# Sampling weights of a deformable convolution: the hats go through DRAM and are spread by DMA, not by selector products

## The chip, the cores and the metric

One core of a Trainium2 chip runs the whole program. The metric is the device time of one execution in microseconds; below is better.

## The reference, cut to what matters

The input is 16 images of 64 channels, 16 x 16 pixels. Four blocks follow each other: (0) a channel attention, x + softmax(q kT / 8) v with a 64 x 64 matrix for each image; (1) a modulated deformable 3 x 3 convolution with batch norm and ReLU; (2) a pixel attention with a 256 x 256 softmax for each image; (3) a block of layer norm, depthwise 3 x 3 convolution, four gated 1-D depthwise scans, a fuse product, a second layer norm and a gated feed-forward part.

The change is about block 1. For each of nine taps and each output pixel it samples the image at a fractional place:

```python
py = off_y + hh[None, None, :, None] + ky[None, :, None, None] - PAD
px = off_x + ww[None, None, None, :] + kx[None, :, None, None] - PAD
sampled = jax.vmap(_bilinear_sample_one)(x, py, px)
sampled = sampled * mask[:, None]
out = jnp.einsum('bckhw,ock->bohw', sampled, w_dcn.reshape(O, C, KK))
```

Bilinear interpolation with zeros outside is the same as a product of two "hats": the weight of source pixel (i, j) is max(0, 1 - |py - i|) * max(0, 1 - |px - j|). So for each tap the kernel builds a matrix of weights, 256 source pixels by 256 output pixels for each image, and lets TensorE multiply it with the image that has already been multiplied with the tap's channel weights.

## The kernel before, in words

Two images make a pair: their 2 x 64 channels fill the 128 partitions, and there are eight pairs. Every pair walks through the same named steps, and a step is written `name.pair`. Each engine works through one written list of steps (`PLAN`), in that order, and waits on semaphores; the lists interleave the steps of several pairs. So an engine's order is fixed, and a step that waits holds everything behind it in its list.

Front steps of pair n: `qk`, `attn`, `at`, `mix`, `x1` (block 0), `off` and `off_t` (offsets, transposed so that pixels are partitions, lines 430 to 447), `wx0` to `wx2` (image times tap weights, line 480). On VectorE `dist` (line 872), on ScalarE `abs`, on VectorE `hat` and `hat_y` make the hats: for each output pixel (a partition) 18 rows of 16 values, y and x for nine taps.

Then the hats must come to the layout that the products need: source pixel as partition, output pixel along the row. Before the change this goes so. ScalarE rounds the hats to fp16 (`high`, line 710), GpSimd computes the low part, again fp16 (`low`, line 1039, for the first pair partly on VectorE, line 891). TensorE transposes both in fp16 (`tr0` to `tr2`, line 464), ScalarE copies them out of PSUM (line 719). For each tap k the step `sp{k}` (lines 504 to 519) makes three products with constant 0/1 selector matrices: two spread the y hats over the partitions, one for each half of the source rows (line 494, banks `yb`), and one spreads the x hats (line 489, bank `xb`). ScalarE copies the x part to SBUF (`xe{k}`, line 740) and VectorE multiplies, once for each half (`w{k}a`, `w{k}b`, line 901). TensorE then accumulates the samples (`s{k}a`, `s{k}b`, line 534) in the bank `cv`, and ScalarE writes the ReLU (line 747). Weights live in a ring of six tiles, the copies of x in three.

Back steps: `qk2`, `v2`, `logit`, `max`, `exp`, `nrm`, `et`, `av` (block 2), then `x3`, `st1`, `ln1`, nine taps `dw` (two on ScalarE, seven on VectorE, line 942), `y`, `gate`, `scan` (line 615), `prod` (line 957), `fuse`, `x4`, `st2`, `ln2`, `ff`, `u`, `ff2`, `out` (block 3). GpSimd computes the layer norms' scale and shift.

The PSUM banks `mb` and `pair` are shared by many steps; `turn` makes a step wait until the one before it in the same bank was read. `warm` and `hot` are products of a zero tile that nobody reads, put where TensorE would wait; `WARM` and `HOT` say how many pairs of them. SP issues the loads of parameters and of x, and the stores of y.

## Time and profile before

| | |
|---|---|
| median of 3 timed runs | 303.65 us (303.19 to 303.67) |
| span of the profiled execution | 301.8 us; its own time is not listed, the median run lies 1.9 us above this span |
| TensorE busy | 287.8 us (95%), 2870 matmuls |
| TensorE weight loads | 183.7 us (61%), beside the matmuls |
| VectorE busy | 213.0 us (71%), 424 instructions |
| ScalarE busy | 190.4 us (63%), 399 instructions |
| GpSimd busy | 53.0 us (18%), 139 instructions |
| DMA | 4.98 MB in all, mean 16 GB/s |
| granted TensorE clock | full speed (2.4 GHz) in all 40 slices |

Busy time is the union of an engine's instructions in the span. Matmuls are pipelined, so that one lasts longer than the time until the next can start: what a step costs a full TensorE is read from the start of the next step, or from the chain of waits, which goes back from the last instruction to what released each piece.

### The profile page before, as it was taken

The page shows a single profiled execution, that of the slowest core. Times are in us where ns is not written, and L with a number is a line of the kernel's source. Part 1 is how long each engine was busy: PE and PEld are TensorE (multiplying, and loading weights), DVE is VectorE, ACT ScalarE, POOL GpSimd, SP SyncE. Part 2 cuts the span into 40 slices and gives each one's busy share as a digit, 9 for nine tenths or more (in the row PEclk, how much of TensorE's full clock was granted, in tenths as well). Part 3 has the DMA queues.
Part 4 walks back from the last instruction along what each step waited for, and adds up shares of the span by engine and source line. Part 5 has one row for each costly group of instructions (what it writes and reads, how often), then busy time and mean ns, then how long its engine had stood idle before and what let it go on. Part 6 is the DMA issues. An engine that isn't in the chain of part 4 may idle for free.

```text
span 301.8 us, 7399 instructions
## 1 busy us (share of the span) xinstructions
PE 287.8 (95%) x2870; PEld 183.7 (61%) x2870; DVE 213.0 (71%) x424; ACT 190.4 (63%) x399; POOL 53.0 (18%) x139
## 2 busy tenths in 40 slices
...
DMA packets 3057, 4.98 MB, mean 16 GB/s; under 512 B 336, under 2 KB 2768, under 8 KB 2896
## 3 DMA queue, kind: packets, MB, share of 16 engines
...
## 4 chain that ended last, share of the span: by engine, by line
PE 85%; DVE 5%; ACT 5%; issue 3%; POOL 1%; ACTq 0%; POOLq 0%; DVEq 0%
PE ps_cv L534 22%; PE ps_pair L615 11%; PE ps_yb L494 8%; PE ps_pair L480 7%; PE ps_ma L437 6%; PE ps_ma L464 4%; PE ps_mb L580 3%; PE ps_pair L602 3%; PE ps_pair L570 3%; PE ps_mb L591 3%; PE ps_mb L547 3%; PE ps_mb L388 2%; PE ps_pair L635 2%; PE ps_mb L624 2%; PE ps_yb L374 1%
## 5 line engine op out<-in xcount | busy, mean ns | idle before, releaser
L901 DVE TENSOR_TENSOR sb_wt<-ps_yb,sb_xe 128x512 f32<-128x512 f32 x144 | 94.0, 684 | 26.4 <-PE ps_xb L489 24.9
L534 PE MATMUL ps_cv<-sb_wt,sb_w_x 128*64 128x256 f32 x576 | 77.3, 385 | 0.0
L740 ACT ACTIVATE sb_xe<-ps_xb 128x512 f32<-128x512 f32 x72 | 43.0, 597 | 19.3 <-PE ps_xb L489 19.2
L534 PEld LDWEIGHTS ps_cv<-sb_wt,sb_w_x 128*64 128x64 f32 x576 | 38.2, 136 | 20.2 <-issue 7.5
L615 PE MATMUL ps_pair<-sb_y_pad,sb_par 64*128 64x256 f32 x320 | 37.4, 383 | 0.3 <-ACT sb_gates L799 0.3
L615 PEld LDWEIGHTS ps_pair<-sb_y_pad,sb_par 64*128 64x128 f32 x320 | 30.9, 184 | 5.8 <-issue 2.5
L942 DVE SCALAR_TENSOR_TENSOR sb_dw_acc<-sb_z_pad,sb_par,sb_dw_acc 128x256 f32<-128x256 f32 x56 | 25.2, 480 | 9.4 <-ACT sb_dw_acc L792 5.3
L494 PE MATMUL ps_yb<-sb_hats,sb_sel 32*128 32x512 f16 x144 | 29.8, 383 | 0.7
L1039 POOL TENSOR_TENSOR sb_parts<-sb_hat,sb_parts 128x256 f16<-128x256 f32 (+2 forms) x40 | 23.3, 615 | 38.7 <-ACT sb_parts L710 38.6
L1046 POOL TENSOR_SCALAR sb_sc<-sb_mv 128x1 f32<-128x1 f32 x16 | 3.0, 190 | 142.1 <-DVE sb_mv L936 74.7
L489 PE MATMUL ps_xb<-sb_hats,sb_sel 32*128 32x512 f16 x72 | 27.7, 385 | 0.2 <-ACT sb_hats L719 0.2
L730 ACT ACTIVATE sb_w_x<-ps_pair 128x1024 f32<-128x1024 f32 (+1 forms) x24 | 19.4, 810 | 7.7 <-PE ps_pair L480 7.5
L480 PE MATMUL ps_pair<-sb_par,sb_x 64*128 64x256 f32 (+1 forms) x192 | 23.4, 361 | 0.6 <-ACT sb_w_x L730 0.3
L719 ACT ACTIVATE sb_hats<-ps_ma 128x1024 f16<-128x1024 f16 (+1 forms) x24 | 21.1, 880 | 1.7 <-PE ps_ma L464 1.5
L494 PEld LDWEIGHTS ps_yb<-sb_hats,sb_sel 32*128 32x128 f16 x144 | 7.3, 91 | 21.2 <-issue 17.0
L480 PEld LDWEIGHTS ps_pair<-sb_par,sb_x 64*128 64x128 f32 x192 | 15.5, 185 | 7.3 <-issue 6.7
L808 ACT ACTIVATE sb_conv<-ps_pair,sb_par 128x512 f32<-128x512 f32 x16 | 10.1, 683 | 13.1 <-PE ps_pair L615 13.0
L437 PE MATMUL ps_ma<-sb_x_pad,sb_par 128*64 128x128 f32 x288 | 17.4, 274 | 0.3 <-ACT sb_hats L719 0.3
L437 PEld LDWEIGHTS ps_ma<-sb_x_pad,sb_par 128*64 128x64 f32 x288 | 15.8, 136 | 2.3 <-issue 1.6
L769 ACT ACTIVATE sb_b_exp<-ps_pair,sb_b_neg 128x256 f32<-128x256 f32 x32 | 14.8, 473 | 3.0 <-DVE sb_b_neg L910 2.7
L872 DVE TENSOR_TENSOR sb_dist<-ps_ma,sb_grid 128x1152 f32<-128x1152 f32 x8 | 10.8, 1354 | 6.2 <-PE ps_ma L446 6.2
L464 PE MATMUL ps_ma<-sb_sel,sb_parts 128*64 128x128 f16 x320 | 13.8, 222 | 0.0
...
## 6 DMA issues: line engine op xcount, KB each, us to landing
sb_par<-in_par SPq DMA_DIRECT2D x1, 1519.5 KB, 7.7
sb_x_in<-in_x SPq DMA_DIRECT2D x8, 128.0 KB, 2.1
out_y<-sb_y_out SPq DMA_DIRECT2D x8, 128.0 KB, 1.7
...
sb_par<-in_par SPq DMA_DIRECT2D x1, 128.0 KB, 2.2
sb_sel<-in_sel SPq DMA_DIRECT2D x1, 128.0 KB, 3.9
```

What stands on the lines that cost most here:

```text
L437: mm = nc.tensor.matmul(ma[C * h:C * (h + 1), 0:P], par_sb[:, a + 2 * OM * t:a + 2 * OM * (t + 1)], x1_pad[:, r:r + HALF_ROWS, t % 3:t % 3 ...
L464: mm = nc.tensor.transpose(bk[columns_of(t), at:at + P], parts[:, 2 * h + b, 4 * g + 2 * t:4 * g + 2 * (t + 1), :, :], ident16)
L480: mm = nc.tensor.matmul(pair[:, 512 * b + PIX * h:512 * b + PIX * h + k], x1[r, P * h:P * (h + 1)], par_sb[r, a:a + k], start=True, stop=True)
L489: return nc.tensor.matmul(xb[:, :], sel_sb[rows, P:2 * P], hats[n % 2][rows, g, :], start=True, stop=True)
L494: return nc.tensor.matmul(yb[h][:, :], sel_sb[rows, P * (2 + h):P * (3 + h)], hats[n % 2][rows, g, :], start=True, stop=True)
L534: mm = nc.tensor.matmul(cv[C * b:C * (b + 1), 0:PIX], w_x[n % 2][:, b, h, k, :], wt_of(n, k, h)[:, PIX * b:PIX * (b + 1)], start=(k == 0 a ...
L615: mm = nc.tensor.matmul(pair[:, 512 * b + PIX * d:512 * b + PIX * (d + 1)], par_sb[r, a:a + P], rows, start=(j == 0), stop=(j == KS - 1))
L719: nc.scalar.activation(hats[n % 2][:, g0:g1, :].rearrange("p g q -> p (g q)"), ma[:, :].bitcast(F16)[:, 0:k], ACT.Copy).then_inc(ev(f"hats ...
L740: nc.scalar.activation(xe[t % XE][:, :], xb[:, :], ACT.Copy).then_inc(ev("xe_ok"), 1)
L901: nc.vector.tensor_tensor(wt_of(n, k, h)[:, :], yb[h][:, :], xe[t % XE][:, :], ALU.mult)\
L942: nc.vector.scalar_tensor_tensor(out=sum_of, in0=dw_source(t), scalar=col("dw_w", t), in1=sum_of, op0=ALU.mult, op1=ALU.add).then_inc(ev(f ...
L1039: nc.gpsimd.tensor_tensor(parts[:, 0:g, a:b, 1, :], hat[:, 0:g, a:b, :], parts[:, 0:g, a:b, 0, :], ALU.subtract).then_inc(ev("low_ok"), 1)
```

## The change

The low and high parts, the selector products, their constants (`in_sel`) and the copies of x go. Instead:

- `tr0` to `tr2` each transpose the f32 hats of three taps, 96 rows, in four blocks of 128 pixels; ScalarE copies them to SBUF in f32.
- SP gets a list of its own. `keep{g}` writes the 96 x 512 block of group g to a DRAM tensor of the program. `ld{k}` reads it back for tap k in three DMAs, each with a source that repeats rows, so that every one of 128 partitions gets a row of 512 f32: once the x hats, and twice (for each half) the y hats. Four such sets of buffers (`SPREADS`).
- `w{k}` is one VectorE product of 128 x 1024 for both halves, the x part broadcast. The ring has three tiles of twice the size.
- "Another layout": source pixels lie on the partitions with x slow and y fast, so that both spreads have an outer dimension of 16; GpSimd's copy of `x1` is permuted to match, in two pieces.
- The three banks that are free now go to a second `cv`, to a bank `mc` of its own for the back steps that shared `mb`, and to `rest` for the filler. Many tiles get a second buffer (`z_pad`, `dw_acc`, `y_pad`, `gates`, `conv`, `prod`, `z2`, `ff_*`), x4 a third, x2 one for each pair, and waits are written for their reuse.
- All lists are written anew.

```diff
-GROUPS = 5
-SLOT = 2 * H
+GROUPS = 3
+GROUP_TAPS = 3
+ROWS = 2 * H * GROUP_TAPS
...
-RING = 6
-HOT = {1: 4, 2: 2, 3: 3, 4: 2, 5: 5, 6: 5, 7: 8, 8: 13, 9: 4}
-WARM = {1: 5, 2: 2, 3: 5, 4: 1, 5: 3, 6: 2, 7: 3}
-XE = 3
+RING = 3
+SPREADS = 4
+HOT = {1: 6, 2: 1, 3: 1, 4: 1, 5: 1, 6: 2, 7: 1, 8: 4, 9: 1, 10: 3, 11: 3, 12: 2, 13: 2, 14: 1, 15: 2, 16: 18, 17: 3, 18: 3, 19: 8, 20: 3}
+WARM = {1: 7, 2: 2, 3: 4, 4: 1, 5: 1, 6: 1, 7: 1, 8: 4, 9: 1, 10: 2, 11: 1, 12: 1, 13: 1}
...
+            def keep(g):
+                def step(n):
+                    sp.wait_ge(ev(f"hats_ok{g}"), n)
+                    if n > 2:
+                        sp.wait_ge(ev("wt_ok"), tap(n - 2, GROUP_TAPS * (g + 1) - 1))
+                    sp.dma_start(hats_d[n % 2][g, :, :], hats[n % 2][:, g, :]).then_inc(kept[g][n % 2], 16)
+                return step
+
+            def spread(k):
+                def step(n):
+                    t, g, r = tap(n, k), k // GROUP_TAPS, 2 * H * (k % GROUP_TAPS)
+                    sp.wait_ge(kept[g][n % 2], 16 * ((n + 1) // 2))
+                    wait_past(sp, ev("wt_ok"), t - SPREADS)
+                    whole = [W, HALF_ROWS, 2 * PIX]
+                    rows = hats_d[n % 2][g, r + H:r + 2 * H, :]
+                    sp.dma_start(xs[t % SPREADS][:, :],
+                                 rows.unsqueeze(1).to_broadcast(whole)).then_inc(landed[t % SPREADS], 16)
+                    for h in range(HALVES):
+                        rows = hats_d[n % 2][g, r + HALF_ROWS * h:r + HALF_ROWS * (h + 1), :]
+                        sp.dma_start(ys[t % SPREADS][:, h, :],
+                                     rows.unsqueeze(0).to_broadcast(whole)).then_inc(landed[t % SPREADS], 16)
+                return step
...
-                    bk = ma[:, :].bitcast(F16)
-                    for g in range(g0, g1):
-                        for b in range(2):
-                            for h in range(HALVES):
-                                at = 2 * PIX * (g - g0) + PIX * b + P * h
-                                for t in range(2):
-                                    mm = nc.tensor.transpose(bk[columns_of(t), at:at + P],
-                                                             parts[:, 2 * h + b, 4 * g + 2 * t:4 * g + 2 * (t + 1), :, :],
-                                                             ident16)
+                    for b in range(2):
+                        for h in range(HALVES):
+                            at = PIX * b + P * h
+                            mm = nc.tensor.transpose(ma[0:ROWS, at:at + P],
+                                                     hat[:, 2 * h + b, 2 * GROUP_TAPS * g:2 * GROUP_TAPS * (g + 1), :], ident)
...
-            def weights(k, h):
+            def weights(k):
                 def step(n):
                     t = tap(n, k)
-                    dve.wait_ge(ev("sp_mm"), spread_of(n, k) + h)
-                    if h == 0:
-                        dve.wait_ge(ev("xe_ok"), t)
-                    wait_past(dve, ev("smp_mm"), slot(n, k, h) - RING)
-                    nc.vector.tensor_tensor(wt_of(n, k, h)[:, :], yb[h][:, :], xe[t % XE][:, :], ALU.mult)\
-                        .then_inc(ev("wt_ok"), 1)
+                    dve.wait_ge(landed[t % SPREADS], 48 * ((t - 1) // SPREADS + 1))
+                    wait_past(dve, ev("smp_mm"), 2 * (t - RING))
+                    nc.vector.tensor_tensor(wt_of(n, k)[:, :, :], ys[t % SPREADS][:, :, :],
+                                            xs[t % SPREADS][:, :].unsqueeze(1).to_broadcast([P, HALVES, 2 * PIX]),
+                                            ALU.mult).then_inc(ev("wt_ok"), 1)
                 return step
```

The parts of the new lists that the prediction speaks of. SP, the first two pairs:

```
load.3 keep0.1 keep1.1 keep2.1 ld0.1 ld1.1 ld2.1 ld4.1 load.4 ld3.1 ld6.1 keep0.2 ld5.1 ld7.1 load.5 ld8.1 ld0.2
```

The end of TensorE's list, from the last samples of pair 8:

```
s8a.8 s8b.8 hot.8 qk2.8 hot.9 gate.7 hot.10 scan.7 hot.11 ff.6 fuse.7 logit.8 ff2.6 hot.12 v2.8 hot.13 et0.8
hot.14 et1.8 hot.15 av.8 hot.16 gate.8 hot.17 scan.8 hot.18 ff.7 fuse.8 hot.19 ff.8 ff2.7 hot.20 ff2.8
```

and as it was before:

```
s8a.8 s8b.8 ff2.5 scan.6 qk2.8 hot.1 logit.8 fuse.6 hot.2 hot.3 v2.8 hot.4 et0.8 gate.7 et1.8 av.8 scan.7 hot.5
ff.6 fuse.7 gate.8 hot.6 scan.8 ff2.6 hot.7 fuse.8 ff.7 hot.8 ff.8 ff2.7 hot.9 ff2.8
```

The end of VectorE's new list, from the last weights:

```
w8.8 x4.6 st2.6 dw2.7 dw3.7 dw4.7 dw5.7 dw6.7 dw7.7 dw8.7 y.7 prod.7 x4.7 u.6 max.8 out.6 nrm0.8 nrm1.8 st2.7 x3.8
```

## Rows read from the trace of the kernel before

**Rows 1.** Busy time of each engine in three stretches, columns as in its header.
```profile
core 0: us, PE busy (x) PEld busy (x) DVE busy (x) ACT busy (x) POOL busy (x), PEclk, DMA share, GB/s
0.00:28.00 28.00, 22.53 (x243) 13.85 (x245) 10.35 (x25) 11.98 (x26) 7.07 (x18) 1.00 0.32 106
28.00:253.00 225.00, 222.79 (x2282) 142.06 (x2282) 179.65 (x350) 158.15 (x334) 38.92 (x96) 1.00 0.02 6
253.00:301.80 48.80, 42.52 (x352) 27.81 (x348) 23.02 (x51) 20.23 (x41) 6.96 (x25) 1.00 0.04 12
```
**Rows 2.** The page's part 4, the chain that ended last, by engine and line.
```profile
PE 85%; DVE 5%; ACT 5%; issue 3%; POOL 1%; ACTq 0%; POOLq 0%; DVEq 0%
PE ps_cv L534 22%; PE ps_pair L615 11%; PE ps_yb L494 8%; PE ps_pair L480 7%; PE ps_ma L437 6%; PE ps_ma L464 4%; PE ps_mb L580 3%; PE ps_pair L602 3%; PE ps_pair L570 3%; PE ps_mb L591 3%; PE ps_mb L547 3%; PE ps_mb L388 2%; PE ps_pair L635 2%; PE ps_mb L624 2%; PE ps_yb L374 1%
```
**Rows 3.** The chain in order of time, 236 to 302: start us, us, what.
```profile
237.12 0.32 PE ps_yb L494 x2
...
237.45 0.34 PE ps_ma L464 x8
...
248.78 0.59 PE ps_mb L580 x4
...
255.56 4.61 PE ps_pair L615 x40
...
261.19 0.86 PE ps_xb L380 x8
```
**Rows 4.** Groups by line: out<-in and shapes xcount | busy us, mean ns | idle before.
```profile
L901 DVE TENSOR_TENSOR sb_wt<-ps_yb,sb_xe 128x512 f32<-128x512 f32 x144 | 94.0, 684 | 26.4 <-PE ps_xb L489 24.9 <-PE ps_yb L494 1.2
L740 ACT ACTIVATE sb_xe<-ps_xb 128x512 f32<-128x512 f32 x72 | 43.0, 597 | 19.3 <-PE ps_xb L489 19.2
L942 DVE SCALAR_TENSOR_TENSOR sb_dw_acc<-sb_z_pad,sb_par,sb_dw_acc 128x256 f32<-128x256 f32 x56 | 25.2, 480 | 9.4 <-ACT sb_dw_acc L792 5.3 <-ACT sb_dw_acc L790 3.5
L957 DVE SCALAR_TENSOR_TENSOR sb_prod<-sb_gates,sb_conv 128x1024 f32<-128x1024 f32 x8 | 9.7, 1218 | 0.3 <-ACT sb_conv L808 0.3
```
**Rows 5.** DMA in the first 20 us: queue's packets, MB, share; issues, KB, landing.
```profile
q1 hardware_dynamic: 1152, 2.81, 42.7%
...
sb_par<-in_par SPq DMA_DIRECT2D x1, 1519.5 KB, 7.7
...
sb_x_in<-in_x SPq DMA_DIRECT2D x3, 128.0 KB, 2.2
```
**Rows 6.** SP's issues in order of time: start us, us, line, what.
```profile
1.15 0.43 SPq L326 DMA_DIRECT2D sb_x_in<-in_x  x1
1.63 0.42 SPq L327 DMA_DIRECT2D sb_par<-in_par  x1
```
**Rows 7.** The head in order of time: start us, us, engine, line, what.
```profile
19.50 0.76 DVE L885 SCALAR_TENSOR_TENSOR sb_hat<-sb_msk,sb_hat 128x576 f32<-128x576 f32 x1
...
27.10 0.69 DVE L901 TENSOR_TENSOR sb_wt<-ps_yb,sb_xe 128x512 f32<-128x512 f32 x1 [1.20 <-PE ps_xb L489]
```
**Rows 8.** The tail in order of time, the same columns.
```profile
252.33 0.69 DVE L901 TENSOR_TENSOR sb_wt<-ps_yb,sb_xe 128x512 f32<-128x512 f32 x1 [0.49 <-PE ps_yb L494]
...
262.31 1.13 PE L570 MATMUL ps_pair<-sb_k,sb_q 64*128 64x256 f32 x8 [0.26 <-issue]
...
280.09 1.16 PE L602 MATMUL ps_pair<-sb_y_pad,sb_par 64*128 64x256 f32 x8 [0.27 <-DVE sb_y_pad L951]
...
281.29 1.26 ACT L799 ACTIVATE sb_gates<-ps_pair,sb_gate_bh 128x512 f32<-128x512 f32 x2 [1.47 <-PE ps_pair L602]
...
295.26 1.13 PE L635 MATMUL ps_pair<-sb_z,sb_par 64*128 64x256 f32 x8
...
299.19 0.48 DVE L984 SCALAR_TENSOR_TENSOR sb_y_out<-ps_mb,sb_par,sb_x 128x256 f32<-128x256 f32 x1 [0.76 <-PE ps_mb L643]
```

More of the change, by code:

```diff
@@ L75 @@
[L75 to L78 removed]
+        warm.1 qk.1 warm.2 attn.1 warm.3 at.1 warm.4 mix.1 warm.5 x1.1 warm.6 off.1 warm.7 off_t.1 wx0.1 prep.1 warm.8
```

455 lines of the change are left out of this document (196 added, 259 removed).

## The prediction, made before the result

> **What bounds the kernel now.** Read first the table of stretches [rows 1]: between 28 and 253 us TensorE is busy 222.8 of 225.0 us while VectorE has 179.7 (80%), ScalarE 158.2 (70%) and the DMA engines 2%. So the long middle costs what TensorE's instructions cost, one behind the other, and an instruction removed there is time removed, as long as its work's replacement arrives in time. The other two stretches are different. Before 28 us one pair walks alone through its chain (only 22.5 us busy, and 42 of its matmuls are filler), and after 253 us, where the last weights are made, 42.5 of 48.8 us are busy, but 92 filler instructions at 0.108 us (eight take 0.86 [rows 3]) are 10 of them: 32 us of real work. Those ends are set by latency. The chain of waits says the same by line [rows 2]: 85% of it is PE, with the spread products (line 494, which stands for the whole trio with line 489) at 8% and the fp16 transposes (line 464) at 4%.
>
> The span is 301.8 us. The median of the timed runs is 303.65, so 1.9 us lie around the span. My sum is made in the span, and 1.9 is added at the end.
>
> **What TensorE loses.** The 216 selector products go as 72 trios. A trio's instructions last 0.39 us each, but they overlap, and what counts is the time until the next step starts: 0.32 us in the chain [rows 3]. 72 x 0.32 = 23.0 us. (The page's 8% is 24.) The chain shows them on the path in the middle, so I take all of it: -23.0.
>
> **What TensorE gains.** 320 fp16 transposes go: 40 a pair, eight take 0.34 us [rows 3], and line 464 has 4% of the chain at most; I take 10.6 us (3.5% of the span, within that rounding). 96 f32 transposes come, 12 a pair in 24 groups of four. The f32 transposes of the attention have nearly this form (four 128x128 blocks): 0.59 us a group [rows 3]; 24 x 0.59 = 14.2. Net +3.6. TensorE altogether: -19.4 us.
>
> **VectorE.** 144 products of 128x512 (684 ns alone, 94.0 us together) become 72 of 128x1024. The product over 128x1024 from SBUF to SBUF takes 1218 ns [rows 4]: 87.7 us, 6.3 less. That product has no broadcast operand; at worst one costs two of the old ones (1368 ns, +4.5 us), at best it overlaps as those did (94.0 / 72 less one fixed cost, about 1150 ns, -11). I take 1218, the row of this size. It is not the bound, but with the middle shorter its share there stays at 80 to 82%.
>
> **ScalarE and GpSimd.** 72 copies of 597 ns [rows 4], the fp16 copy of the hats and the double-width copies behind the transposes go; 24 copies of 96x512 come. ScalarE is covered by TensorE before and after: 0. The same for GpSimd's low parts, except in the head, where they stand between hat and transpose. Double buffers and the separate PSUM bank for the second half take away waits that TensorE at 99% busy hardly shows: 0, at best -1.5.
>
> **What DMA has to bring.** A tap now needs three copies of 128x512 f32: 0.786 MB; 72 taps are 56.6 MB against 4.98 now. No row shows a broadcast read of DRAM. Bounds: in the first 20 us 1152 packets moved 2.81 MB at 42.7% of 16 engines [rows 5], so 0.329 MB/us at full use: 2.4 us a tap. The slow end is the 1519.5 KB load, 7.7 us from issue to landing [rows 5], 0.202 MB/us: 3.9 us a tap. A fast end below 2.4 brings nothing more. Issue is no limit: SP starts a transfer every 0.47 us [rows 6], 1.4 us a tap. I take 2.4, the row that counts engine time. A pair then needs 9 x 2.4 + 1.8 for writing 0.59 MB + 0.8 for x and y = 24.2 us, and a pair of the new middle lasts (244.7 - 28.2) / 8 = 27.1 us. It fits, at 89%. Four buffers cover a latency of about 2.2 us (x load [rows 5]) plus two taps.
>
> The SP queue is in one written order: a spread waits for the weights four taps back, and behind it stand the next pair's writes, x loads and stores. The x loads are far ahead and the stores are awaited two pairs later, so nothing but taps waits for it. In pair 1 the order holds ld3 behind ld4 and a load, so its taps come no faster than one in about 2.4 us; the pair took from 27.1 to some 51 us before, 2.7 a tap, so that is covered too.
>
> **The head.** Before: hat ready at 20.3, weights of tap 0 at 27.10 [rows 7]. After: hat ready at about 20.0 (its DVE steps are ahead of qk.2), then three rounds of transposes and copies (0.66 + 0.7 each) to 24.1, because ld0 stands behind keep2; three issues to 25.9; the tap's data 2.4 us from 24.9, and about 1 us to the receipt: 28.2. +1.1 us.
>
> **The tail.** This is where the new order gives time back. Before, the last weights end at 253.0, logit.8 starts at 262.31, and the span ends at 301.8 [rows 8]. After, the order puts logit.8 behind gate.7, scan.7, ff.6 and fuse.7. From the end of w8.8: x4.6, st2.6 and seven dw steps (480 ns each, less when back to back [rows 4]) and y.7 to 5.1; gate.7 to 6.4 and its two activations to 7.7; scan.7 4.61 [rows 3] to 12.4; its activations to 13.8; ff.6 to 14.9, its two to 16.4 (durations of these forms [rows 8]); logit.8 at 16.7 instead of 9.3. From there the chain is 39.5 as before less prod.7 (1.2) and gate.7 (0.4), which now come earlier: 37.9. Tail 54.6 instead of 48.8. In exchange scan.6 (4.61) and 24 matmuls of fuse.6, av.7, ff2.5 and the sampling (at 0.108: 2.6) now lie before the last weights: 7.2 us.
>
> **The fill.** The new order has 13 pairs of filler matmuls in the middle (hot.1 to hot.7). 26 instructions take 2.8 us. They cost nothing if TensorE waits there anyway, which is then itself a loss, so I count 2.8 either way.
>
> **Sum.** Last weights at 253.0 - 23.0 + 3.6 + 7.2 + 1.1 + 2.8 = 244.7; tail 54.6: span 299.3; plus 1.9: 301.2 us. Most of 19.4 us saved is thus given back: 5.8 + 7.2 by the tail, 3.9 by head and fill.
>
> **Rivals.**
> A, the broadcast reads are slow. All 16 engines read the same 2 KB row of DRAM one after the other. From 2.75 us a tap on supply sets the pace: (9 x 2.75 + 2.6) x 8 = 219 us behind 28.2, last weights at 247, time 303.6, and all beyond is slower than before. Half way to the slow end, 3.15 us a tap, a pair takes 31: 28.2 + 248 + 54.6 + 1.9 = 333; at the end itself some 390. For it: nothing of this kind was measured before, and 89% use leaves little. Against: the packets of different rows ran at full engine rate. The Trainium skill (DMA: Bandwidth & Descriptors, Latency and other measured facts) tells of lock-stepped per-partition streams that fell from about 214 to 103 GB/s, with channel aliasing only inferred; as an estimate 103 GB/s would be 7.6 us a tap. No row here bears on that. 20%.
> B, order and waits. VectorE at 82%, TensorE full and taps at 89% in three fixed queues wait for each other: between w8.7 and w8.8 VectorE has some 21.5 us of work and TensorE 22.7, so each wait shows. If 4% of the 217 us is lost, +8.7: 310. Of the same size is a fall of the granted clock in the thinner tail (gate.8 and scan.8, 5.8 us at full clock, would take 11.6: 307). The granted clock is 1.00 in all stretches, the 2.4 GHz level, the tail included [rows 1]; but there scan.7 stood in the gap before gate.8 where now only filler stands. The Trainium skill (TensorE: Matmul & The Clock Gate, HAM oscillation) says that waits between bursts of matmuls bring the 1.2 GHz level back. 20%.
> C, the tail's estimate is too long, or the middle gives up its waits. If the tail and the fill cost nothing more, 303.65 - 19.4 = 284.3. For it: 19.4 us are certain work removed. Against: the written order of logit.8. 18%.
>
> **Chances.** My forecast 42%, its own range 295 to 308 (of it 28 faster, 5 same, 9 slower); A 20, B 20 (1 faster, 4 same, 15 slower), C 18. 0.2% is about what can be told from no change. Faster 0.47, same 0.09, slower 0.44. The range leaves out the end of C and the upper half of A: 286 to 325.
>
> **What would show it.** PE busy falls by about 19 us without filler. DMA share about 60% in the middle, the three copies of a tap landing within 4 us of issue. If VectorE's weights wait for DMA for more than 10 us in all, A holds. The last weights near 245 and logit.8 near 261 show tail and middle right; weights past 250 with short DMA waits show B. Wrong altogether: the last product of weights ends before 238, or a 128x1024 product with a broadcast operand takes over 1.4 us.

## The result: slower by 5.6%, where 0.8% faster was forecast

The changed kernel takes 320.91 us (median of 4 runs, 319.11 to 322.3), the kernel before 303.66 beside it: ratio 1.0559, 95% interval 1.0529 to 1.0589. Forecast was 301.2. The time lies outside the forecast's own range (295 to 308), inside the whole range (286 to 325), and on the slow side of the kernel before, where the fast side was forecast. The profiled run has a span of 320.4 us and a time of its own of 322.3, so 1.9 us lie around the span, as before.

First the table of stretches of the changed kernel, which answers to [rows 1] (its last weights end at 262.7):

```profile
core 0: us, PE busy (x) PEld busy (x) DVE busy (x) ACT busy (x) POOL busy (x), PEclk, DMA share, GB/s
0.00:30.00 30.00, 23.80 (x228) 13.67 (x230) 10.27 (x26) 8.65 (x23) 5.18 (x15) 1.00 0.48 150
30.00:55.00 25.00, 22.12 (x222) 14.20 (x218) 15.53 (x20) 9.63 (x21) 1.85 (x2) 0.93 0.99 252
55.00:100.00 45.00, 41.35 (x388) 26.61 (x386) 32.31 (x56) 22.37 (x65) 3.98 (x9) 0.96 1.00 282
100.00:150.00 50.00, 49.53 (x482) 34.86 (x478) 43.74 (x69) 27.10 (x59) 8.54 (x17) 1.00 1.02 281
150.00:200.00 50.00, 48.56 (x436) 33.76 (x436) 38.95 (x63) 25.66 (x57) 11.45 (x24) 1.00 0.95 264
200.00:250.00 50.00, 41.62 (x338) 27.39 (x334) 34.33 (x59) 23.15 (x50) 5.97 (x15) 1.00 0.96 249
250.00:262.70 12.70, 10.94 (x92) 6.80 (x94) 10.95 (x19) 3.52 (x11) 1.03 (x1) 1.00 0.72 197
262.70:320.40 57.70, 40.69 (x313) 25.16 (x308) 19.48 (x45) 18.57 (x37) 6.98 (x25) 0.93 0.02 8
```

The DMA share, forecast at about 60% in the middle, is 0.95 to 1.02 from 30 to 250 us: the 16 engines are busy all the time. TensorE is no longer full: outside its busy time lie 320.4 - 278.6 = 41.8 us, against 301.8 - 287.8 = 14.0 before. TensorE lost nearly the work that the forecast took from it. With fp16 hats (e3 below) its busy time is 274.9. 26 more filler pairs, 52 instructions of 0.108 us, are 5.6 of that, so 287.8 - 274.9 + 5.6 = 18.5 us went, against 19.4. What was saved came back as waiting.

The groups by line that the forecast priced, and two of GpSimd that it had as covered (out<-in and shapes, count | busy us, mean ns | idle before):

```profile
L848 DVE TENSOR_TENSOR sb_wt<-sb_ys,sb_xs 128x1024 f32<-128x1024 f32 x72 | 87.1, 1224 | 21.6 <-DMA sb_ys<-hats_d 14.2 <-PE ps_cv L496 7.0 <-issue 0.3
L467 PE MATMUL ps_ma<-sb_par,sb_hat 128*96 128x128 f32 x96 | 15.8, 288 | 0.6 <-ACT sb_hats L675 0.2
L996 POOL TENSOR_SCALAR sb_sc<-sb_mv 128x1 f32<-128x1 f32 x16 | 9.6, 598 | 182.4 <-DVE sb_mv L887 111.0 <-DVE sb_mv L925 71.2
L988 POOL COPY sb_x<-sb_x_pad 128x128 f32<-128x128 f32 x16 | 8.2, 590 | 71.4 <-PE ps_pair L482 71.4
```

VectorE's product takes 1224 ns, as forecast; it waits 14.2 us for the spread rows, over the 10 us that were named as the sign of rival A. GpSimd's first scalar operation of a LayerNorm takes 598 ns on average; the same operation before, from the groups by line of GpSimd:

```profile
L1046 POOL TENSOR_SCALAR sb_sc<-sb_mv 128x1 f32<-128x1 f32 x16 | 3.0, 190 | 142.1 <-DVE sb_mv L936 74.7 <-DVE sb_mv L972 67.5
```

The timeline shows how it is stretched. VectorE first, then GpSimd (start us, us, engine, line):

```profile
157.87 1.22 DVE L848 TENSOR_TENSOR sb_wt<-sb_ys,sb_xs 128x1024 f32<-128x1024 f32 x1
166.43 2.36 DVE L848 TENSOR_TENSOR sb_wt<-sb_ys,sb_xs 128x1024 f32<-128x1024 f32 x2
```

```profile
158.21 0.93 POOL L1001 TENSOR_TENSOR sb_sc<-sb_sc,sb_par 128x1 f32<-128x1 f32 x1
159.21 0.19 POOL L1003 TENSOR_TENSOR sb_sc<-sb_mv,sb_sc 128x1 f32<-128x1 f32 x1
166.60 1.11 POOL L996 TENSOR_SCALAR sb_sc<-sb_mv 128x1 f32<-128x1 f32 x1 [6.93 <-DVE sb_mv L887]
```

The operation begun at 158.21 ends at 159.14, 50 ns behind the product beside it (159.09); the next, beside no such product but a tensor_scalar of 128x256 (line 870, from 159.19), takes 0.19. The one begun at 166.60 ends at 167.71, again 50 ns behind the first of two products. GpSimd waits for VectorE's product to end. The Trainium skill (SBUF — State Buffer, SBUF: two separate sides) has a rule for it: a VectorE operation with two SBUF inputs, or in a two-port performance mode, holds a port pair that a GpSimd operation reading SBUF needs, for its whole length. The trace agrees for two SBUF inputs: the product of before read one operand from PSUM, and GpSimd's operation took 190 ns.

The head ends with VectorE's first product of weights:

```profile
29.53 0.23 DVE L801 TENSOR_REDUCE sb_a_max<-ps_mb 128x1 f32<-128x64 f32 x1 [1.04 <-PE ps_mb L407]
29.79 0.15 DVE L803 TENSOR_SCALAR sb_a_neg<-sb_a_max 128x1 f32<-128x1 f32 x1
30.37 1.22 DVE L848 TENSOR_TENSOR sb_wt<-sb_ys,sb_xs 128x1024 f32<-128x1024 f32 x1 [0.42 <-DMA sb_ys<-hats_d]
```

It starts at 30.37, where 28.2 was forecast. The hats were copied by 23.7 and the three transfers issued by 26.0, as forecast; but VectorE's new list has `w0.1` behind `x1.2` and `a_max.3`, which end at 29.94, and the transfers end another 0.4 us later.

Last the tail, PE in order of time; it answers to [rows 8]:

```profile
280.32 1.14 PE L532 MATMUL ps_pair<-sb_k,sb_q 64*128 64x256 f32 x8 [0.22 <-ACT sb_ff_g L776]
...
288.94 4.08 PE L389 MATMUL ps_rest<-sb_idle 128*64 128x512 f16 x36
296.98 2.08 PE L564 MATMUL ps_pair<-sb_y_pad,sb_par 64*128 64x256 f32 x8 [3.96 <-DVE sb_y_pad L902]
298.99 1.49 PE L389 MATMUL ps_rest<-sb_idle 128*64 128x512 f16 x6
300.52 5.37 PE L577 MATMUL ps_pair<-sb_y_pad,sb_par 64*128 64x256 f32 x40
```

logit.8 starts 17.6 us behind the last weights (forecast 16.7; 9.3 before). Behind a wait of 3.96 us gate.8 takes 2.08 us, where [rows 8] has 1.16, and scan.8 5.37. The granted clock is 0.93 in this stretch, a mean of the levels of 2.4 and 1.2 GHz, and was 1.00 before.

### The profile page after: what moved, and what is told of

Read it like the earlier page. It is cut to its first block, busy times and chain, and to the rows that moved or that the text cites. A ratio compares the mean times of both kernels' runs of the same rounds, so it can differ in the third digit from the quotient of the medians.

```text
span 320.4 us, 6653 instructions
## 1 busy us (share of the span) xinstructions
PE 278.6 (87%) x2482; PEld 182.5 (57%) x2482; DVE 205.6 (64%) x352; ACT 138.6 (43%) x319; POOL 45.0 (14%) x107
## 3 DMA queue, kind: packets, MB, share of 16 engines
q1 hardware_dynamic: 36672, 65.75, 74.7%
## 4 chain that ended last, share of the span: by engine, by line
PE 40%; DVE 18%; DMA 13%; issue 8%; ACT 7%; SPq 6%; POOL 6%; DVEq 0%; ACTq 0%; POOLq 0%
DMA sb_ys<-hats_d 13%; PE ps_pair L577 7%; PE ps_cv L496 7%; DVE sb_wt L848 5%; SPq L349 4%; PE ps_ma L446 3%; PE ps_pair L482 3%; DVE sb_dw_acc L893 3%; PE ps_ma L467 2%; PE ps_mb L397 2%; PE ps_pair L532 2%; PE ps_pair L564 2%; SPq L345 2%; POOL sb_sc L999 2%; DVE sb_dist L827 2%
## 5 line engine op out<-in xcount | busy, mean ns | idle before, releaser
L848 DVE TENSOR_TENSOR sb_wt<-sb_ys,sb_xs 128x1024 f32<-128x1024 f32 x72 | 87.1, 1224 | 21.6 <-DMA sb_ys<-hats_d 14.2
L496 PEld LDWEIGHTS ps_cv<-sb_wt,sb_w_x 128*64 128x64 f32 x576 | 38.8, 137 | 27.3 <-issue 14.2
L577 PE MATMUL ps_pair<-sb_y_pad,sb_par 64*128 64x256 f32 x320 | 38.1, 388 | 1.6 <-ACT sb_gates L751 1.6
L996 POOL TENSOR_SCALAR sb_sc<-sb_mv 128x1 f32<-128x1 f32 x16 | 9.6, 598 | 182.4 <-DVE sb_mv L887 111.0
L909 DVE SCALAR_TENSOR_TENSOR sb_prod<-sb_gates,sb_conv 128x1024 f32<-128x1024 f32 x8 | 9.8, 1224 | 20.8 <-ACT sb_conv L760 20.8
L720 ACT ACTIVATE sb_b_exp<-ps_pair,sb_b_neg 128x256 f32<-128x256 f32 x32 | 14.8, 471 | 13.3 <-DVE sb_b_neg L859 13.3
L675 ACT ACTIVATE sb_hats<-ps_ma 96x512 f32<-96x512 f32 x24 | 14.1, 588 | 13.5 <-PE ps_ma L467 13.4
L389 PE MATMUL ps_rest<-sb_idle 128*64 128x512 f16 x132 | 18.8, 393 | 0.0
L988 POOL COPY sb_x<-sb_x_pad 128x128 f32<-128x128 f32 x16 | 8.2, 590 | 71.4 <-PE ps_pair L482 71.4
L446 PE MATMUL ps_ma<-sb_x_pad,sb_par 128*64 128x128 f32 x288 | 17.4, 273 | 0.7 <-DVE sb_x_pad L818 0.6
L751 ACT ACTIVATE sb_gates<-ps_pair,sb_gate_bh 128x512 f32<-128x512 f32 x16 | 10.1, 684 | 17.0 <-PE ps_pair L564 17.0
L446 PEld LDWEIGHTS ps_ma<-sb_x_pad,sb_par 128*64 128x64 f32 x288 | 16.0, 136 | 2.4 <-DVE sb_x_pad L818 1.4
L467 PE MATMUL ps_ma<-sb_par,sb_hat 128*96 128x128 f32 x96 | 15.8, 288 | 0.6 <-ACT sb_hats L675 0.2
L467 PEld LDWEIGHTS ps_ma<-sb_par,sb_hat 128*96 128x96 f32 x96 | 9.8, 130 | 9.6 <-issue 6.6
L564 PE MATMUL ps_pair<-sb_y_pad,sb_par 64*128 64x256 f32 x64 | 10.2, 437 | 5.7 <-DVE sb_y_pad L902 4.7
```

Source lines behind the costliest of these rows:

```text
L389: nc.tensor.matmul(rest[C * t:C * (t + 1), :], idle[:, C * t:C * (t + 1)], idle[:, :], start=True, stop=True)
L446: mm = nc.tensor.matmul(ma[C * h:C * (h + 1), 0:P], par_sb[:, a + 2 * OM * t:a + 2 * OM * (t + 1)], x1_pad[:, r:r + HALF_ROWS, t % 3:t % 3 ...
L467: mm = nc.tensor.transpose(ma[0:ROWS, at:at + P], hat[:, 2 * h + b, 2 * GROUP_TAPS * g:2 * GROUP_TAPS * (g + 1), :], ident)
L496: mm = nc.tensor.matmul(cv[n % 2][C * b:C * (b + 1), 0:PIX], w_x[n % 2][:, b, h, k, :], wt_of(n, k)[:, h, PIX * b:PIX * (b + 1)], start=(k ...
L564: mm = nc.tensor.matmul(pair[:, 512 * b + PIX * d:512 * b + PIX * (d + 1)], par_sb[r, a:a + P], y_pad[n % 2][r, 2:2 + H, 2:2 + W], start=T ...
L577: mm = nc.tensor.matmul(pair[:, 512 * b + PIX * d:512 * b + PIX * (d + 1)], par_sb[r, a:a + P], rows, start=(j == 0), stop=(j == KS - 1))
```

## Experiments

Three theories stood at the start. Supply: the transfers set the pace (rival A). Order: the written order makes the tail long, or makes engines wait for each other (rival B). Hold: GpSimd's held operations, which the forecast had at nothing. Behind e4 a fourth is added, clock: the fall of the granted clock ahead of gate.8. The intervals are of the ratio to the kernel before, in the same session (medians 303.2 to 304.4 us).

| kernel | us | ratio, 95% interval |
|---|---|---|
| changed kernel | 320.91 | 1.0559 (1.0529 to 1.0589) |
| e1 one copy of ys | 313.36 | 1.0329 (1.0294 to 1.0364) |
| e2 distinct rows | 312.83 | 1.0316 (1.0301 to 1.0331) |
| e3 fp16 hats | 312.01 | 1.0288 (1.0271 to 1.0305) |
| e4 three-operand product | 321.45 | 1.0593 (1.0557 to 1.0629) |
| e5 one SBUF input, fp16 | 306.55 | 1.0095 (1.0067 to 1.0122) |
| e6 tail order, fp16 | 300.63 | 0.9898 (0.9872 to 0.9923) |
| e7 more filler, fp16 | 312.92 | 1.0291 (1.0246 to 1.0337) |
| e8 tail order, f32 | 307.65 | 1.0123 (1.0075 to 1.0171) |
| e9 scan.6 behind the samples, fp16 | 298.96 | 0.9857 (0.9825 to 0.9889) |
| e10 one input, padded, fp16 | 311.01 | 1.0239 (1.0215 to 1.0262) |
| e11 row pitch, f32 | 306.15 | 1.0092 (1.0059 to 1.0126) |
| e12 scan.6 and pitch, f32 | 312.42 | 1.0265 (1.0206 to 1.0323) |
| e13 no filler, fp16 | 323.36 | 1.0645 (1.0593 to 1.0696) |
| e14 PSUM operand, no filler, fp16 | 315.20 | 1.0367 (1.0333 to 1.0401) |
| e15 norm on ScalarE, on e9 | 299.94 | 0.9878 (0.9850 to 0.9906) |
| e16 norm on ScalarE, fp16 | 313.90 | 1.0348 (1.0311 to 1.0386) |
| e17 norm on ScalarE, on e8 | 310.00 | 1.0208 (1.0165 to 1.0252) |

e1, e2, e5, e10 and e14 leave out or replace a part of the weights, so they show times and are no kernels to keep. The fp16 forms keep the hats in one fp16 rounding, where the kernel before had a high and a low part.

### e1 to e3: the transfers

e1, two copies of a tap in place of three:

```diff
-                    for h in range(HALVES):
+                    for h in range(1):
-                    dve.wait_ge(landed[t % SPREADS], 48 * ((t - 1) // SPREADS + 1))
+                    dve.wait_ge(landed[t % SPREADS], 32 * ((t - 1) // SPREADS + 1))
```

> The changed kernel, but each tap is spread by two DMAs instead of three: the second copy of the y hats is left out and both halves use the first (so the y weights of the lower half are wrong). Traffic per tap 0.524 MB instead of 0.786, everything else the same. Supply theory (the 16 DMA engines at 2.86 us a tap set the pace of the middle): the last weights, at 262.7 us now, come near 246, and the time falls from 321 to 303-307. Order theory (three fixed queues and their waits cost the 18 us, whatever DMA does): last weights stay past 258 and the time at 316-321. DMA share of the middle about 65-70%.

e2, the same bytes from 128 distinct rows of in_par:

```diff
-                                 rows.unsqueeze(1).to_broadcast(whole)).then_inc(...)
+                    sp.dma_start(xs[t % SPREADS][:, :], par[:, 0:2 * PIX]).then_inc(...)
```

> The changed kernel, but the three DMAs of a tap read 128 different rows of 2 KB of the parameter tensor instead of one row of the kept hats 8 or 16 times (so the weights are other numbers); same bytes, same waits, same writes. Hot-row theory (a 2 KB packet takes 119 ns in the mean and not 84 because many engines read the same DRAM rows): packets near 85-90 ns, 2.1 us a tap, time 303-308. Load theory (the engines are simply full, whatever the row): packets stay near 119 ns and the time within 1% of 321.

e3, hats, their copy in DRAM, xs and ys in fp16, so half the bytes in as many transfers:

```diff
-        xs = [sb(f"xs{i}", [P, 2 * PIX]) for i in range(SPREADS)]
+        xs = [sb(f"xs{i}", [P, 2 * PIX], F16) for i in range(SPREADS)]
```

> The changed kernel with the kept hats and the spread tiles in fp16 (written so by ScalarE's copy out of PSUM); the product still writes f32. Half the bytes in packets of 1 KB, as many packets and DMAs. Supply theory: near 1.2-1.5 us a tap, no waits for DMA, last weights near 245, time 302-306. Order theory: 316-321. If packets and not bytes were the limit, nothing would change either.

All three come out within 1.4 us of each other, 7.6 to 8.9 us under the changed kernel. The queue of the spreads (packets, MB, share of 16 engines) in the changed kernel, e2 and e3:

```profile
q1 hardware_dynamic: 36672, 65.75, 74.7%
```

```profile
q1 hardware_dynamic: 36672, 65.75, 63.5%
```

```profile
q1 hardware_dynamic: 36672, 35.07, 37.9%
```

At full use that is 65.75 / (0.747 x 320.4) = 0.275 MB/us in the changed kernel, so 0.786 / 0.275 = 2.86 us a tap; from distinct rows 65.75 / (0.635 x 311.1) = 0.333, 2.36 us a tap, the 2.4 of the forecast. A packet of 2 KB takes 119 ns on average in the one and 97 in the other. A lighter load does not remove it: e1 has two thirds of the spread transfers and a share of 52.4%, and still moves 46.87 / (0.524 x 312.5) = 0.286 MB/us. VectorE's wait for the rows falls from 14.2 us to 3.2 in e2 and 0.2 in e3:

```profile
L845 DVE TENSOR_TENSOR sb_wt<-sb_ys,sb_xs 128x1024 f32<-128x1024 f32 x72 | 86.6, 1223 | 9.1 <-PE ps_cv L493 5.5 <-DMA sb_ys<-in_par 3.2 <-issue 0.3
```

```profile
L848 DVE TENSOR_TENSOR sb_wt<-sb_ys,sb_xs 128x1024 f32<-128x1024 f16 x72 | 86.5, 1223 | 6.2 <-PE ps_cv L496 5.5 <-issue 0.3 <-DMA sb_ys<-hats_d 0.2
```

So supply is worth 8.9 us in this order, and no more: with the wait for it gone, 312.0 is left, and in all three the last weights end at 253 to 254 us. Something else sets them there. Part of it may be the head: in e3 the first product starts 1.9 us behind the forecast's 28.2, without a wait for transfers.

```profile
30.11 1.22 DVE L848 TENSOR_TENSOR sb_wt<-sb_ys,sb_xs 128x1024 f32<-128x1024 f16 x1
```

### e4: the form of the product

```diff
-                    nc.vector.tensor_tensor(wt_of(n, k)[:, :, :], ys[...], xs[...], ALU.mult)
+                    nc.vector.scalar_tensor_tensor(out=wt_of(n, k)[:, :, :], in0=ys[...], scalar=1.0,
+                                                   in1=xs[...], op0=ALU.mult, op1=ALU.mult)
```

> The changed kernel with the weights' product as scalar_tensor_tensor, (y * 1.0) * x, instead of tensor_tensor: the same result, both inputs still in SBUF. GpSimd's one-column operations of the layer norms grew from 190 to 598 ns in the mean (line 996) and end with a product of VectorE that runs beside them. If that is special to tensor_tensor, they return to 190 ns and the time falls by 2 to 5 us. If it comes from two inputs in SBUF, nothing changes: 598 ns, within 0.5% of 321. Supply theory and order theory both: no other change.

The time stays: product 1223 ns, GpSimd's first operation 667. Another instruction with the same operands holds GpSimd as well.

### e5 to e8: one operand, order, clock

e5:

```diff
-                    nc.vector.tensor_tensor(wt_of(n, k)[:, :, :], ys[...], xs[...], ALU.mult)
+                    nc.vector.tensor_scalar(wt_of(n, k)[:, :, :], ys[...], col("bn", 0), None, ALU.mult)
```

> Hats in fp16 (as e3_fp16_hats, 312.0 us) and the weights as tensor_scalar of ys alone by a per-partition constant: the x operand is left out of the weights (it is still transferred). VectorE's wide product has one operand in SBUF in place of two. Theory lock (two SBUF operands of VectorE hold back GpSimd's small operations): L996 on GpSimd falls from 655 ns mean to about 190 to 220 ns, L999 from 730 to about 550, the copies L988 from 584 to about 415; if this bounds the back end of pairs 5 to 7 the time falls by 3 to 6 us, to 306 to 309 us, with PE's idle time between 200 and 240 us halved. Rival (GpSimd is late for another reason, such as the stage's load): the means stay over 450 ns. Rival (lock there, but covered by the order of the work): the means fall and the time stays at 310 to 312.5 us. The product itself may become shorter, near 0.7 to 0.85 ns per column by the 0.76 us of L832 with 1152 columns; that alone is worth little, since VectorE idles a third of the span.

306.55, at the lock theory's figure, but for a mixed reason. Two groups of e5:

```profile
L848 DVE TENSOR_SCALAR sb_wt<-sb_ys,sb_par 128x1024 f32<-128x1024 f16 x72 | 52.7, 751 | 10.1 <-PE ps_cv L496 8.7 <-DMA sb_ys<-hats_d 0.9 <-issue 0.3
L994 POOL TENSOR_SCALAR sb_sc<-sb_mv 128x1 f32<-128x1 f32 x16 | 6.1, 380 | 178.9 <-DVE sb_mv L885 108.8 <-DVE sb_mv L923 69.9
```

GpSimd's mean is 380, not 190: the shorter operation with one SBUF input holds it too, 617 to 637 ns where they meet. And VectorE's products take 34 us less. e10 was made to part the two.

e6, the tail in the order of the kernel before (likewise on ScalarE, VectorE, GpSimd and in the filler counts):

```diff
-        s8a.8 s8b.8 hot.8 qk2.8 hot.9 gate.7 hot.10 scan.7 hot.11 ff.6 fuse.7 logit.8 ff2.6 ...
+        s8a.8 s8b.8 hot.8 qk2.8 hot.9 logit.8 hot.10 v2.8 hot.11 et0.8 gate.7 et1.8 hot.12 av.8 scan.7 ...
```

> Hats in fp16 and, from the last sample of pair 8 on, the order of the steps of the kernel before (logit.8 straight after qk2.8, gate.7, scan.7, ff.6 behind it, ln1.8 ahead of ln2.7 on GpSimd, filler counts of before). Theory order (the tail is long because logit.8 stands behind gate.7, scan.7 and ff.6 in the order for the pair bank): logit.8 comes about 5 us after the last weights in place of 17.6 (9.3 before), the tail falls from 57.7 to 49 to 51 us and the time from 312.0 to 304 to 306 us. Rival (the tail is long because more back-end work of pairs 6 and 7 is left for it): the tail stays at 55 us or more, the time at 309 to 312. Rival (clock): if only the clock fall goes, 310 us.

The order theory, and more than it said: 11.4 us. The last weights end at 253.0, as in e3; VectorE, then PE, of e6:

```profile
251.75 1.23 DVE L848 TENSOR_TENSOR sb_wt<-sb_ys,sb_xs 128x1024 f32<-128x1024 f16 x1
```

```profile
254.70 1.93 PE L389 MATMUL ps_rest<-sb_idle 128*64 128x512 f16 x16
256.65 1.08 PE L509 MATMUL ps_mc<-sb_x,sb_par 128*64 128x256 f32 x8
257.56 1.03 PE L389 MATMUL ps_rest<-sb_idle 128*64 128x512 f16 x8
258.78 1.13 PE L532 MATMUL ps_pair<-sb_k,sb_q 64*128 64x256 f32 x8 [0.18 <-issue]
...
276.77 1.16 PE L564 MATMUL ps_pair<-sb_y_pad,sb_par 64*128 64x256 f32 x8 [0.27 <-DVE sb_y_pad L902]
```

logit.8 starts 5.8 us behind the last weights, and the tail lasts 298.6 - 253.0 = 45.6 us in place of 57.7. gate.7, scan.7 and ff.6 stand in the waits of pair 8's chain, so gate.8 does not meet a long one: it takes 1.16 us.

e7:

```diff
-HOT = {..., 16: 18, ...}
+HOT = {..., 16: 36, ...}
```

> Hats in fp16 and 36 filler pairs in place of 18 at hot.16, ahead of gate.8. Theory clock (the 3.9 us in which PE waits ahead of gate.8 lowers the clock, and gate.8 and scan.8 then take 2.08 and 5.37 us against 1.16 and 4.68): granted clock 1.0 all through, gate.8 at 1.16, scan.8 at 4.68, and the time 1.5 to 2 us shorter, 310 to 310.5 us. Rival (filler delays gate.8): filler of 8 us ends after y.8 is ready, the time stays or grows by up to 1 us. Rival (nothing): within 0.2% of 312.0.

The time is no shorter. PE ahead of gate.8, in e3 and in e7:

```profile
279.30 4.08 PE L389 MATMUL ps_rest<-sb_idle 128*64 128x512 f16 x36
287.34 2.08 PE L564 MATMUL ps_pair<-sb_y_pad,sb_par 64*128 64x256 f32 x8 [3.96 <-DVE sb_y_pad L902]
```

```profile
280.30 7.97 PE L389 MATMUL ps_rest<-sb_idle 128*64 128x512 f16 x72
288.35 1.16 PE L564 MATMUL ps_pair<-sb_y_pad,sb_par 64*128 64x256 f32 x8
290.96 4.69 PE L577 MATMUL ps_pair<-sb_y_pad,sb_par 64*128 64x256 f32 x40 [0.69 <-ACT sb_gates L751]
```

The clock is kept and gate.8 and scan.8 take their old lengths. From the start of the filler to the end of scan.8 it is 15.4 us in place of 17.0 (in e3 scan.8 ends at 296.2, here at 295.6), so the clock theory's 1.5 to 2 us are there. The time does not show them: this run lies 1.0 us later already ahead of the filler (280.30 against 279.30), from the head, where unchanged instructions (the offsets, L446) took 2.91 us in place of 2.19 at a granted clock of 0.94 over the first 30 us. The four runs spread from 310.69 us, at a granted clock of 0.999, to 313.88, at 0.982. What the filler gives in the tail is less than these runs differ by.

e8, e6's order in the f32 kernel:

> The changed kernel as it is, hats in f32, with the tail order of the kernel before only. Theory order: the last weights stay at 262.7 us and the tail falls by as much as in the fp16 kernel, 7 to 9 us: 312 to 314 us against 320.9. Rival (the tail's length is set by work left over): 318 to 321 us. If the tail order and the fp16 hats are two separate causes, their gains add: the difference of this kernel to the changed one is the same, within 1 us, as that of the fp16 pair.

13.3 us. The gains add roughly: order is worth 13.3 us in f32 and 11.4 in fp16, supply 8.9 in the changed order and 7.0 in e6's. Together they give 20.3 us, more than the 17.3 by which the changed kernel is slower, so e6 comes under the kernel before.

### e9 to e12: what else lies ahead of the last weights

e9, on e6 (with ScalarE and VectorE accordingly):

```diff
-        ff.5 qk2.7 gate.6 s0a.8 s0b.8 scan.6 ... et1.7 s4b.8 et0.7 ... fuse.6 s6a.8 ... s8b.8 hot.8 qk2.8 ... logit.8
+        ff.5 qk2.7 s0a.8 s0b.8 ... et1.7 s4b.8 gate.6 et0.7 ... s6a.8 ... s8b.8 scan.6 qk2.8 ... logit.8 fuse.6
```

> The fp16 kernel with the tail order of before (e6_tail_order_fp16, 300.6 us), and in it scan.6 behind the last sample of pair 8, fuse.6 behind logit.8, gate.6 four samples later, as in the kernel before. Theory (the work of the back end that is put ahead of the last weights costs its full time there, and only filler time behind them): 5.8 us of PE work (scan.6 4.7, fuse.6 1.1) leaves the stretch ahead of the last weights, which end at 247 to 248 us in place of 253.0; the tail grows by 2 to 4 us from 45.6, as scan.6 takes the place of 8 filler pairs (1.8 us) and of a wait of 1.3 us; time 297 to 299.5 us. Rival (the tail's chain takes all of it back): 300 to 302 us. Rival (pair 7's chain gets later with prod.6): over 302 us.

298.96, the fastest kernel here, 1.4% under the kernel before (and, like e6, with hats of one fp16 rounding). The last weights end at 248.9 (4.1 us earlier), the tail is 47.9 (2.3 longer).

```profile
247.64 1.23 DVE L848 TENSOR_TENSOR sb_wt<-sb_ys,sb_xs 128x1024 f32<-128x1024 f16 x1
```

e10:

```diff
+                    nc.vector.memset(spare[t % SPREADS][:, :], 0.0)
                     nc.vector.tensor_scalar(wt_of(n, k)[:, :, :], ys[...], col("bn", 0), None, ALU.mult)
```

> As e5_one_sbuf_input (hats in fp16, order as in the changed kernel, the x operand left out of the weights; 306.55 us), with a memset of 128x450 ahead of each product, so that VectorE is busy about as long per tap (0.46 + 0.75 us) as with the product of two operands (1.22 us). It tells apart the two things e5 changed at once. Theory lock (two SBUF operands held GpSimd back, and this cost the time): GpSimd's means stay near those of e5 (380 ns for the first scalar operation, 490 for the copies, against 655 and 584), and the time at 306 to 308 us. Rival (e5 gained by VectorE's 34 us less of work alone): the time goes back to 311 to 312.5 us, GpSimd's means whatever they are.

It missed its purpose: GpSimd is held by the memset as well, an operation begun beside it ending 50 ns behind the tensor_scalar that follows. GpSimd's first operation:

```profile
L997 POOL TENSOR_SCALAR sb_sc<-sb_mv 128x1 f32<-128x1 f32 x16 | 10.3, 644 | 178.3 <-DVE sb_mv L888 108.6 <-DVE sb_mv L926 69.4
```

With GpSimd held for as long as in e3 (655) and VectorE nearly as busy (193.5 against 204.7 us, e5 173.2), the time is back at 311.0. Which of the two gave e5 its 5.5 us is not told.

e11, on e8:

```diff
-        hats_d = [nc.dram_tensor(f"hats_d{i}", (GROUPS, ROWS, 2 * PIX), F32, ...
+        hats_d = [nc.dram_tensor(f"hats_d{i}", (GROUPS, ROWS, PACK), F32, ...
```

> The f32 kernel with the tail order of before (e8_tail_order_f32, 307.65 us), the rows of the hats in DRAM 17,892 bytes apart, as those of in_par were in e2_distinct_rows, in place of 2,048. Each row is read as often as before. Theory repeated rows (a 2 KB packet takes 119 ns because 8 or 16 partitions read the same row at once): packets stay at 115 to 120 ns, queue share over 70%, time 307 to 308.5 us. Rival (the packed rows lie in the same part of the memory, and it is their closeness that costs): packets fall to 97 to 100 ns, time 301 to 304 us, waits of VectorE on the transfers from 16 to about 3 us.

Mostly repeated rows: 115 ns a packet (119 in e8, 97 in e2), 65.75 MB at 76.2% of 304.0 us, so 0.284 MB/us. The 1.5 us off the time are within the spread of its 8 runs (304.7 to 308.7).

e12, e9's order and e11's pitch in f32:

> The changed kernel in f32 with all that the orders and the row pitch gave: the tail order of before, scan.6, gate.6 and fuse.6 later (as e9_scan6_behind_samples, -1.7 us in fp16) and rows 17,892 bytes apart (as e11_row_pitch_f32, 306.15 us). If the two gains add: 304 to 305 us, still 0.3 us or more over the kernel before. Rival (the DMA queues bound the stretch ahead of the last weights, so that PE work moved out of it frees nothing): 305.5 to 307 us, last weights at 257 to 259 us. Rival (the work moved lets the transfers run ahead): under 303.5 us, faster than before.

Wrong on all sides: 312.4, 6.3 us over e11. The profiled run is its fastest, at 309.7; there the last weights end at 259.9 against 258.3, the wait for rows is 15.4 us against 12.7, and the tail is 2.2 us longer, as in e9. Why the work moved out of that stretch frees nothing there stays open. The two profiled runs differ by 3.9 us; e12's other three runs are 2.3 to 4.1 us slower than its profiled one, at a lower granted clock (0.978 to 0.984 against 0.994). No f32 form came under the kernel before.

### e13 to e17: the price of the hold

e13, e3 without any filler, all counts of `HOT` and `WARM` at 0:

> The control of the next run: e3_fp16_hats (312.0 us) without any filler matmuls (warm and hot counts 0). PE's clock will fall where it waits, in the first 30 us and behind the last weights above all, so the time rises, by 5 to 20 us: 317 to 332 us. GpSimd's first scalar operation stays near 650 ns.

e14, on e13 (the constant block is written once by TensorE):

```diff
-                    nc.vector.tensor_tensor(wt_of(n, k)[:, :, :], ys[...], xs[...], ALU.mult)
+                    nc.vector.tensor_tensor(wt_of(n, k)..., ys[...],
+                                            rest[:, 0:PIX].unsqueeze(1).to_broadcast([P, 2 * HALVES, PIX]), ALU.mult)
```

> As e13_fp16_no_filler, but the x operand of the weights is a constant block in the PSUM bank that the filler used (the x part of the weights is left out), so that VectorE's product has one operand in SBUF and one in PSUM, as in the kernel before, and about the same duration, 1.2 to 1.3 us. Theory hold: VectorE's product no longer holds GpSimd: the first scalar operation falls from 650 to 190 ns but beside the depthwise steps. If the hold is part of the 9 us that the transfers don't explain, the time is 3 us or more under e13; rival (the hold is covered by the order, as the forecast had it at nothing): within 1 us of e13; rival (the PSUM operand makes the product longer): L848's mean over 1.3 us and the time over e13.

e13 takes 323.36 us. With e14 it is the pair that decides. Two groups of e14:

```profile
L854 DVE TENSOR_TENSOR sb_wt<-sb_ys,ps_rest 128x1024 f32<-128x1024 f16 x72 | 85.9, 1215 | 5.6 <-PE ps_cv L501 4.9 <-issue 0.3 <-DMA sb_ys<-hats_d 0.2
L1003 POOL TENSOR_SCALAR sb_sc<-sb_mv 128x1 f32<-128x1 f32 x16 | 3.4, 215 | 185.9 <-DVE sb_mv L894 112.9 <-DVE sb_mv L932 72.9
```

The product lasts as long as ever (1215 ns), GpSimd's operation 215 in place of 655: 15 of 16 take about 190 ns and one 580, beside `u` (line 937), a product of two SBUF operands. The time falls by 8.2 us, 323.36 to 315.20; the last weights end at 252.2 in place of 257.8 (5.6 us), the tail is 61.0 in place of 63.4. The product's own 7 ns are 0.5 us of 72.

The tail has to be taken apart, since behind the last weights no such product runs. GpSimd, then PE, of e13 and of e14:

```profile
256.72 1.11 POOL L996 TENSOR_SCALAR sb_sc<-sb_mv 128x1 f32<-128x1 f32 x1 [23.24 <-DVE sb_mv L887]
264.05 1.64 PE L564 MATMUL ps_pair<-sb_y_pad,sb_par 64*128 64x256 f32 x8 [0.72 <-DVE sb_y_pad L902]
267.14 6.72 PE L577 MATMUL ps_pair<-sb_y_pad,sb_par 64*128 64x256 f32 x40 [1.45 <-ACT sb_gates L751]
```

```profile
251.12 0.19 POOL L1003 TENSOR_SCALAR sb_sc<-sb_mv 128x1 f32<-128x1 f32 x1 [23.23 <-DVE sb_mv L894]
257.54 1.16 PE L569 MATMUL ps_pair<-sb_y_pad,sb_par 64*128 64x256 f32 x8
```

The last product of weights holds ln1.7's first operation for 0.9 us, and gate.7 starts 6.3 us behind the last weights in place of 5.4. So 5.6 + 0.9 = 6.5 us are the hold itself. The other 1.5 or so go with the granted clock (0.74 in e13's tail, 0.77 in e14's): gate.7 and scan.7 are slower in e13 and scan.8 in e14. That part belongs to kernels without filler. In the kernel as it is the pair can't be made, since the filler uses that PSUM bank; its ln1.7 is held by the same 0.9 us (1.11 us at 261.67).

e15 to e17 take three of the five small operations off GpSimd (on e9, e3 and e8):

```diff
-                    nc.gpsimd.tensor_tensor(scl[:, 2:3], scl[:, 1:2], col(gain, 0), ALU.mult).then_inc(ev(g_ok), 1)
+                nc.scalar.activation(scl[:, 2:3], scl[:, 1:2], ACT.Copy, scale=col(gain, 0)).then_inc(ev(f"g{i}_ok"), 1)
```

> The same move alone, on e3_fp16_hats (312.0 us; order of the changed kernel). Theory hold: 308 to 310 us. Rival: within 1 us of 312.

> The fastest form so far (e9_scan6_behind_samples, fp16, 298.96 us), with the last three of the five small operations of each LayerNorm taken from GpSimd to ScalarE, ahead of the activation that uses them. Theory hold (GpSimd's small operations are held until VectorE's product ends, 655 in place of 190 ns at the first, and this costs up to 8 us, as e13 to e14): two operations can be held in place of five, 2 to 4 us off, 295 to 297 us. Rival (ScalarE's three operations of about 0.2 us cost as much as GpSimd's did: in the tail they stand on the chain): 298.5 to 300 us.

> The same move on e8_tail_order_f32 (307.65 us; hats in f32, tail order of before). Theory hold: 304 to 306 us, so the f32 form comes within 1% of the kernel before but not under it. Rival (there the transfers set the pace ahead of the last weights, and only the tail gains): 306.5 to 308 us.

All three are slower than what they were built on, by 1.9, 1.0 and 2.4 us. In e16 the two operations that stay are held as before, and ScalarE's take 0.29 us each, where GpSimd's unheld ones take 0.19, and stand in ScalarE's order:

```profile
L1007 POOL TENSOR_SCALAR sb_sc<-sb_mv 128x1 f32<-128x1 f32 x16 | 10.5, 654 | 192.0 <-DVE sb_mv L898 117.0 <-DVE sb_mv L936 74.9
L736 ACT ACTIVATE sb_sc<-sb_sc,sb_par 128x1 f32<-128x1 f32 x16 | 4.7, 292 | 18.1 <-POOL sb_sc L1010 18.1
```

The fix failed; it says nothing against the hold, which it left in place.

## Why the prediction was wrong

**Right.** TensorE's savings (-19.4; 18.5 measured with fp16 hats). The transposes: 96 of them, 15.8 us busy, 0.66 a group where 0.59 was taken. VectorE's product (1218; 1224). The 1.9 us around the span.

**What DMA has to bring: the step that failed first.** "I take 2.4, the row that counts engine time." That rate holds for distinct rows (2.36 in e2). For rows that 8 or 16 partitions read, a tap takes 2.86 us. That is past the 2.75 from which, by rival A, supply sets the pace, and A's mechanism is what happened in the middle. With 2.86 A's own sum gives last weights at 254.9 and 311.4 us, 10.2 over the forecast; the measured price is 8.9 us. What makes a repeated row slow is not shown. The strong form of A did not come: no rate fell to a half, as the Trainium skill (DMA: Bandwidth & Descriptors, Latency and other measured facts) tells of streams at large row pitches. Its slow pitches are 4 MiB and more, which no run here has; here a pitch of 17,892 bytes in place of 2,048 changed 119 ns to 115.

**ScalarE and GpSimd: "GpSimd's low parts ... covered", 0.** The step asked what GpSimd loses, not what its remaining work meets. The operand that moved from PSUM to SBUF made each product hold GpSimd, whose LayerNorm operations lead to gate, scan and ff of pairs 1 to 7. Without filler that is 6.5 us (e13 to e14), 5.6 of it ahead of the last weights. In the kernel with filler and f32 hats its price was not measured: there GpSimd is held as well (598 ns), but supply sets the pace beside it. Rival B named mutual waits of this size, without the cause.

**The head.** Forecast 28.2 for the first weights, measured 30.37 (e3: 30.11). The term left out where `w0.1` stands in VectorE's new list, behind `a_max.3`; before, `w0a.1` stood ahead of it. "About 1 us to the receipt" has no row: the first tap's transfers were over at 30.37, 4.4 us behind their last issue. No run puts `w0.1` ahead, so how much of the 1.9 to 2.2 us reaches the end is open.

**The tail.** Forecast 54.6, measured 57.7. Of the 3.1, 0.9 are the hold at the last weights: it brings logit.8 to 17.6 where 16.7 was forecast, and e14, without it, has 16.7. Another 1.6 are gate.8 and scan.8 at the lower clock (e3 to e7). 0.6 are open. The chain of the tail was thus read rightly, and it is the order that is dear: its cost was taken as 5.8 us, and the runs show 11.4 to 13.3, since the old order needs only 45.6 us behind the new middle. The forecast took the old tail as 48.8 whatever was left for it. That did not move the forecast's sum, but it hid what a better order would give.

**The sum.** The profiled span is 320.4 us (this run lies 1.4 above the median), the forecast's 299.3: 21.1 us. The last weights end at 262.7 in place of 244.7. Of these 18.0 us, 9.6 go when supply goes (e3: 253.1). Of the 8.4 left, up to 5.6 are the hold (shown without filler), 1.9 stand in the head, not tested, and 0.9 are open. The tail adds 3.1. The terms were taken one at a time and need not add: supply alone is worth 8.9 in one order and 7.0 in another. Rival C's 284 was not reached by any kernel.
